# Four cross-attention layers on one core: own orders for the last pairs, low parts on VectorE, an earlier wait for the transposes

## What is computed

```
q = hidden_states @ Wq            # 128 x 1024
k, v = enc @ Wk, enc @ Wv         # 77 x 1024 each
probs = softmax(q k^T / 8 + col_bias)     # per head, 128 x 77
out = (probs @ v) @ Wo + bo + hidden_states
```

## Time and profile before

| | us |
|---|---|
| median of 3 runs | 1819.43 |
| lowest, highest | 1819.06, 1823.53 |
| profiled execution, its own time | 1819.92 |
| its span, first to last instruction | 1817.5 |

### The profile page before, as it was taken

How to read it: one execution, slowest core, us unless ns; L and a number is a source line. 1 busy time by engine, 2 the same in 40 slices (tenths; PEclk the granted TensorE clock), 3 DMA queues, 4 the chain that set the end, 5 groups by cost and what they waited for, 6 DMA issues and landing times.

```text
span 1817.5 us, 72896 instructions
## 1 busy us (share of the span) xinstructions
PE 1760.4 (97%) x28400; PEld 1510.9 (83%) x28400; DVE 1578.3 (87%) x3010; ACT 1471.7 (81%) x2987; POOL 1599.4 (88%) x2136
## 2 busy tenths in 40 slices
PE   6599999999999999999999999999999999999996
PEld 6478888888888888888888888888888888888885
DVE  6689988899889998899888998899888898889983
ACT  4388888888888888888888888888888888888873
POOL 3389999999999999999999998999999999999973
PEclk7599999999999999999999999999999999999998
DMA  5269999999999999999999999998999999999996
GB/s 173 43 134 191 174 181 191 186 185 170 192 185 184 183 171 186 193 179 185 176 187 189 177 187 180 187 188 171 189 183 186 183 174 183 178 170 188 174 186 130
DMA packets 1168210, 320.35 MB, mean 176 GB/s; under 512 B 1140246, under 2 KB 1164124, under 8 KB 1167868
## 3 DMA queue, kind: packets, MB, share of 16 engines
q1 hardware_dynamic: 1167868, 315.69, 94.0%
HBM read 15.93 MB, written 4.19 MB: 11 GB/s over the span
## 4 chain that ended last, share of the span: by engine, by line
PE 90%; issue 1%; DMA 1%; SPq 1%; ACT 0%; DVE 0%; ACTq 0%; DVEq 0%
PE ring L1226 50%; PE sc L1368 12%; PE o_ps L1226 9%; PE o_ps L1386 5%; PE ring L1440 5%; PE sc L1347 4%; PE ring L1297 2%; PE sc L1366 1%; PE ring L1421 1%; PE ring L1437 1%; DMA arena<-p_sm 1%; PE ring L1274 0%; PE o_ps L1382 0%; PE ring L1277 0%; SPq L485 0%
## 5 line engine op out<-in xcount | busy, mean ns | idle before, releaser
L1226 PE MATMUL ring<-ctx_four,m_w 128*128 128x154 f16 x6144 | 461.4, 230 | 1.5 <-ACT o_tf L710 0.9
L1226 PEld LDWEIGHTS ring<-ctx_four,m_w 128*128 128x128 f16 x6144 | 428.8, 96 | 2.5 <-ACT o_tf L710 1.3
L1107 DVE TENSOR_TENSOR arena<-sc,row_max 128x616 f32<-128x616 f32 (+1 forms) x384 | 387.0, 1008 | 7.0
L644 POOL TENSOR_TENSOR p_sm<-arena,p_sm 128x616 f16<-128x616 f32 x256 | 334.6, 1318 | 39.5 <-ACT p_sm L710 38.0
L639 POOL TENSOR_TENSOR p_sg<-arena,p_sg 128x512 f16<-128x512 f32 (+1 forms) x256 | 341.9, 1357 | 2.3 <-ACT p_sg L710 2.3
L710 ACT ACTIVATE arena<-ring 128x462 f16<-128x462 f32 (+1 forms) x384 | 198.9, 518 | 153.9 <-PE ring L1226 153.5
L1086 DVE TENSOR_TENSOR arena<-ring,arena 128x462 f16<-128x462 f32 (+1 forms) x384 | 224.6, 586 | 73.2 <-ACT arena L710 64.2
L1226 PE MATMUL ring<-wv_m,ctx_four 128*103 128x512 f16 (+1 forms) x1152 | 281.1, 380 | 0.9 <-ACT v_all L710 0.9
L671 POOL TENSOR_TENSOR arena<-arena 128x1024 f16<-128x1024 f32 x128 | 272.8, 2131 | 9.3 <-ACT arena L710 9.3
L1368 PE MATMUL sc<-arena,x_s 128*128 128x512 f16 (+1 forms) x1152 | 263.6, 338 | 0.0
L1104 DVE TENSOR_REDUCE row_max<-sc 128x6 f32<-128x462 f32 (+2 forms) x384 | 210.9, 576 | 12.1 <-PE sc L1368 11.5
(11 more groups left out here) (172 smaller groups left out, 3682.0 us busy)
## 6 DMA issues: line engine op xcount, KB each, us to landing
v_fourth<-v_tile SPq DMA_DIRECT2D x64, 105.6 KB
ctx_nat<-in_ctx_dram SPq DMA_DIRECT2D x64, 77.0 KB
x_nat<-in_x_dram SPq DMA_DIRECT2D x64, 64.0 KB, 2.4
arena<-p_sg SPq DMA_TRANSPOSE x256, 3.5
arena<-p_sm SPq DMA_TRANSPOSE x256, 4.4
out_dram<-y_out SPq DMA_DIRECT2D x64, 64.0 KB, 2.2
v_fourth<-v_tile SPq DMA_DIRECT2D x32, 101.6 KB
arena<-in_L_xattn_Wk_dram SPq DMA_DIRECT2D x2, 1024.0 KB, 6.0
```

Of the source, the lines that this page charges most:

```text
L644: pool.tensor_tensor(p_sm[:, k, LO, :, 0:S], probs_m[:, hs, :], p_sm[:, k, HI, :, 0:S], ALU.subtract).then_inc(sems["pm_lo"], 1)
L1107: dve.tensor_tensor(out, s_view[:, hs, :], row_max[:, hs].unsqueeze(2).to_broadcast([P, hs.stop - hs.start, S]), ALU.subtract).then_inc(do ...
L1226: ins = pe.matmul(out, a, b, start=(n == 0), stop=(n == len(passes) - 1))
```

## The change

1. `turn_m(m, first half)` waits for om_raw of item m - 2 with count 1 (14 heads done) and not 2 (all 16). This holds in all rounds. The second half still waits for count 2.
2. `output_m` of layer 3 waits for turned_o after the two residual matmuls, not ahead of them. This too holds in all rounds.
3. `pair(NIT, 0)` stays. `pair(NIT, 1)` to `pair(NIT, 5)` are replaced on SP, ACT, DVE and PE by `last_pair`, with other orders. On POOL `pair` stays.
4. The low parts of items 3 and 5 (`low_part`, two halves each, and `low_out`) go from POOL to DVE (`on_vector`).

SP, and its `last_pair`:

```diff
-                    sp.wait_ge(sems["om_raw"], at("om_raw", it, m - 2, 2))
+                    sp.wait_ge(sems["om_raw"], at("om_raw", it, m - 2, half + 1))
...
+            def last_pair(it, n):
+                m = 2 * n + 1
+                if exists(it, m - 2):
+                    turn_m(it, m - 2, 1)
+                if exists(it, m):
+                    turn_m(it, m, 0)
+                if exists(it, m - 4):
+                    turn_out(it, m - 4)
+                if exists(it, m) and part(m) != 3:
+                    move_values(it, m)
+                if layer(m - 6) == LAYERS - 1 and exists(it, m - 6):
+                    store(it, m - 6)
```

POOL (the same condition stands ahead of the two `low_part`), and then a piece of ACT's `last_pair`:

```diff
-                if exists(it, m - 4):
+                if exists(it, m - 4) and not on_vector(it, m - 4):
                     low_out(it, m - 4)
...
+                if exists(it, m):
+                    exponential_m(it, m, 0)
+                    if n == 1:
+                        high_m(it, m, 0)
+                    exponential_m(it, m, 1)
+                if n > 1 and exists(it, m - 4):
+                    normalise_rest(it, n, m - 4)
+                if n > 1 and exists(it, m):
+                    high_m(it, m, 0)
+                if n > 1 and exists(it, m - 4):
+                    high_out(it, m - 4)
+                if exists(it, m):
+                    high_m(it, m, 1)
+                if n > 1:
+                    last_layer(it, n, m - 6)
```

DVE, and PE's `output_m`:

```diff
+            def low_part(it, m, k):
+
+                hs = slice(k * HALF, (k + 1) * HALF)
+                dve.wait_ge(sems["pm_hi"], at("pm_hi", it, m, k + 1))
+                dve.tensor_tensor(p_sm[:, k, LO, :, 0:S], probs_m[:, hs, :], p_sm[:, k, HI, :, 0:S],
+                                  ALU.subtract).then_inc(sems["pm_lo"], 1)
...
-                pe.wait_ge(sems["turned_o"], at("turned_o", it, m, 16))
...
                 pe.wait_ge(sems["xb"], at("xb", it, m, 1))
                 pe.matmul(ring[:, b, 0:D], x_b[st][:, :], ident_y[:, :], start=True, stop=False)
+                pe.wait_ge(sems["turned_o"], at("turned_o", it, m, 16))
```

99 lines of the change are left out of this document (90 added, 9 removed).

## The result

The changed kernel takes 1823.07 us (median, 1821.76 to 1825.70) beside 1819.91 us for the kernel before on the same chip: ratio 1.0017, 95% interval [1.0011, 1.0024], so about 3.2 us more. The forecast was 1821.0 us, the range 1818.2 to 1823.8 us.

A forecast was written before the change was run, and what follows sets the result against it. TensorE's own pace bounds the rounds; in the last 45 us SyncE's single queue of transposes does. turn_out(5) 1.25 us late, less 0.77 us, is +0.5; one slow transpose at +1.1 makes +1.6: 1821.0 us, range 1818.2 to 1823.8.

The forecast's parts named there:

- The rounds, and the relaxed wait: Before the tail: no effect and no new TensorE wait; in the tail the relaxed wait saves turn_m(5, first) 0.2 to 0.3 us.
- The queue: SyncE's queue in the tail: turn_m(3, second) issued 0.5 us late, turn_out(1) 5.2 us late, turn_out(5) 1.25 us late.
- slow transpose: Tail's chain of seven transposes: one counted as slow, at +1.1 us (bounds: none, 0; two, 2.2).
- The start of the chain: SyncE's queue: item 3's low parts done at 1785.1, turn_m(3, first) at 1784.4, 1.9 us gained; each transpose holds it 1.6 us.
- The landing of turn_m(3, second): Tail: it lands 3.9 us after its issue at 1789.7, at 1793.6, and the 18 matmuls end at 1794.3.
- output_m(1): TensorE's tail: 1.9 us after turn_out(1) lands at 1800.1, part of it at the lower clock; values_m(5) starts after it.
- The last round trip: End of tail: ym_raw at 1809.0 and low_out(5) at 1808.9 release turn_out(5) at 1809.15; early residual matmuls gain 0.77 us.
- Rival A: TensorE's tail: the clock falls earlier, in the new gaps; +2.6 us in all, +2.2 if only at the second gap; 33%.
- B: TensorE's tail: the clock doesn't fall before the last product, so faster than before, -0.8 us, 1818.6 us; 10%.
- C: Tail's chain: two or more slow transposes, or a DVE low part waiting for POOL's low_out(1); +3 to +4 us; 9%.
- Low parts on VectorE: Items 3 and 5 in the tail: 0.80 us per low part, 1.22 us per output low part; POOL's 1.32 and 2.13.

The follow-up runs named there:

- x1_waits: The kernel before with only the relaxed wait for 14 heads and the residual matmuls ahead of the wait, all orders old: ratio 0.9992 to the kernel before.
- x2_out_first: The changed kernel with turn_out of an item issued ahead of turn_m(., first) of the next on SyncE's queue: ratio 1.0001 to the kernel before.
- x9_filled_less: The changed kernel with unused matmuls (14, 24, 4 and 12) ahead of the waits for turn_out of items -1, 1, 3, 5: ratio 1.0013 to the kernel before.
- x5_act_early: The changed kernel with ScalarE doing the older item first and VectorE its last two heads' reciprocal ahead of its maxima: ratio 1.0014 to the kernel before.
- x6_best: The changed kernel with ScalarE's and VectorE's older work first, turn_out ahead of the next turn_m(., first), move_values and stores moved: ratio 0.9982 to the kernel before.
- x3_low_on_pool: The changed kernel with low parts and output low parts of items 3 and 5 back on GpSimd: ratio 1.0022 to the kernel before.
- x12_rest_first: x6_best with item 1's last two heads multiplied ahead of scores_m(5) and their reciprocal earlier on VectorE: ratio 0.9977 to the kernel before.
- x10_best_shifted: x6_best with 92 empty TensorE instructions at the start, dropped in building, so a repetition of x6_best: ratio 0.9987 to the kernel before.
- x13_rest_shifted: x12_rest_first with 28 one-row, one-column matmuls (56 instructions) at the start of TensorE's program: ratio 0.9981 to the kernel before.

## Why the prediction was right in sign and range, and where its steps were off

**The rounds, and the relaxed wait.** Right: no new wait of TensorE, and x1_waits shows that the two edits cost nothing. In the tail turn_m(5, first) waits at the relaxed line for the 18 matmuls, as predicted.

**The queue.** Right in mechanism, and confirmed by x2_out_first: turn_out(-1) behind turn_m(3, first), turn_m(3, second) late though its data is ready, turn_out(1) behind turn_m(5, first). In the prediction's axis (0.69 us added to the times of the changed kernel) turn_m(3, first) went at 1785.05 (1784.4 predicted), turn_out(-1) at 1786.8 (1786.2), turn_m(3, second) at 1790.6 (1789.7), turn_out(1) at 1798.96 (1796.2), turn_out(3) at 1805.7 (1802.5) and turn_out(5) at 1812.5 (1809.15).

**Where 2.3 us were missed.** The tail grew by 3.9 us, the forecast said 1.6. turn_out(5) went 3.35 us behind its place in the forecast's timeline; 1.1 us of that the forecast had apart, as its slow transpose, which leaves 2.25 us. Four terms were mis-sized, all to the same side. (a) The start of the chain, 0.9 us by turn_m(3, second): VectorE had done both low parts of item 3 at 1785.6, not 1785.1, turn_m(3, first) went 0.65 us later, and turn_out(-1) held the queue for 2.12 us instead of 1.6. The durations of the low parts were right (VectorE's rows of the changed kernel, two low parts and one output low part):

```profile
1783.39 1.54 DVE L1267 TENSOR_TENSOR p_sm<-arena,p_sm 128x616 f16<-128x616 f32 x2
...
1803.29 1.22 DVE L1273 TENSOR_TENSOR arena<-arena 128x1024 f16<-128x1024 f32 x1 [6.21 <-ACT arena L728]
```

(b) The landing of turn_m(3, second): 4.2 us, not 3.9. It was so in all seven kernels where move_values and a store are issued right ahead of it (4.18 to 4.29 us). (c) The slow transpose: I added it as one lump of 1.1 us at the end. turn_m(5, first) took 5.24 us to land, 1.4 us over the usual, and held the queue for 3.07 us instead of 1.6, so that turn_out(1), and not only what waits for the landing, came 1.5 us late: 0.4 us over the lump. (d) output_m(1): the forecast put 1.9 us between the landing of turn_out(1) and its end, and it took 2.8 us, since all of it ran at the lower clock; the values of item 5 stand behind it, and the chain that ended last leads through both. That is 0.9 us; 0.3 us of it came back on the way to turn_out(5), where the forecast had allowed more for semaphores and for the second condition. With 0.9, 0.3, 0.4 and 0.6 us that is 2.2 of the 2.25 us.

The last round trip was seen wrongly in one more point. The forecast let both conditions of turn_out(5) meet, the output product of item 3 at 1809.0 and the low part at 1808.9. output_m(3) ran at full clock in 1.51 us and was done at 1810.2 us in the changed kernel's own time, the low part at 1811.6: the second alone released it.

Term (c) is no property of the change. In its repetition no transpose of the tail was slow, and turn_out(5) still went 3.6 us later than before. There the 18 matmuls ahead of turn_m(5, first) ran at the lower clock, 1.17 us instead of 0.73. And the kernel before had slow transposes on its own chain (turn_m(5, first) took 5.0 and turn_m(5, second) 4.7 us; x1_waits without them is 0.7 us earlier at turn_out(5)), which the forecast did not set against its own 1.1 us. That the time still fell into the range is owed to its width.

**Rival A.** Its mechanism came true: the clock fell at the end of the gap from 1786.7 to 1790.0 us, as the Trainium skill says in "TensorE: Matmul & The Clock Gate" (HAM oscillation) of gaps between bursts that wait for a DMA; this trace agrees. Its price was about right: of the two terms that I put for it, the 18 matmuls (0.5 us) are there in the repetition (0.44 us) and not in the change's trace, and output_m(1) (0.7 us) is there in both (0.9 us). The estimate from x9_filled_less is 1.1 us in sum. The forecast, which had the clock at full until 1800, I gave 45%, and A 33%; by the profile A was what happened, and its +2.6 us lie nearer to the measured 3.2 us than the forecast's +1.6 us.

**Rivals B and C.** The last product took 2.74 us, so B is out. The time, 3.2 us over before, lies in the band of C (+3 to +4), but neither of C's mechanisms is in the profile: one transpose of the chain was slow, none in the repetition, and VectorE's low parts did not wait for GpSimd's low_out(1), which started at 1792.15, between them.

**What I did not see.** ScalarE's order. I took high_out(1) to be done in time because turn_out(1) was queued late anyway; that was true for this kernel, and the reason why x5_act_early gained so little, but it is half of what the change gives away against x6_best.

**Low parts on VectorE.** Their durations were right to 0.02 us, and the gain of 1.9 us at turn_m(3, first) was counted against the kernel before, where move_values stood in front of it. x3_low_on_pool, where turn_m(3, first) goes at the same point with GpSimd's low parts, shows that the engine had no part in it.

## What to carry to other kernels

In a queue that issues in order, put an issue whose data is ready early ahead of one that waits for newer work, and look at each engine's own order for the second such inversion: it shows only when the first is mended. A faster engine for a step pays only where that engine doesn't have to wait for the step's input. The edits here are worth at most 7 us in 1820, and a single profile of the same program moves a named instruction by 1 us, by where an instruction packet falls beside a transpose and in which stretch the clock is low. So judge such an edit by both, the place of a named instruction and the median of many runs, and repeat the kernel that the conclusion rests on.

## What the runs showed of the hardware

**A transpose with an instruction packet in its flight takes longer.** q8 has 228 packets of 16 KB (227 in two of the traces), TensorE 58,309 instructions: one packet for each 256. In the tails of the fourteen traces (from 1770 us on) I could pair 142 transposes of 512 KB with issue and landing. The 103 with no packet from 0.5 us ahead of their issue to their landing took 3.63 to 4.29 us; the 16 with a packet 0.9 to 2.8 us after their issue all took 4.87 to 5.72 us. Of the other 23, which had a packet at another time, 17 took 4.2 us or less. The slower six: two with a packet 0.5 and 0.7 us after their issue (4.5 us), three right behind a long one with the packet at their issue (4.7 to 5.1 us), and turn_out(1) of x12_rest_first (packet 3.4 us after the issue, 5.65 us). So the expectation of x10_best_shifted, that all transposes of over 4.9 us had their packet 0.9 to 2.7 us after the issue, was too simple. With ten of the sixteen, that issue or the next held the queue for 2.6 to 3.6 us instead of 1.6.

The rounds agree. From 110 to 1765 us of the fourteen traces, turn_m (arena<-p_sm) had a median of 4.03 us without a packet (1,509 of them) and 5.30 us with one 0.9 to 2.8 us after the issue (534); turn_out (arena<-arena) 3.79 us (492) and 5.38 us (404). Two comparisons go beyond such a count: x13_rest_shifted moved the packets by about 53 instructions and turn_out(1) became 1.5 us shorter, and in the two executions of the changed program the same transpose took 5.2 us with the packet 1.2 us behind its issue and 3.8 us with it ahead.

**The clock.** The 24 matmuls of an output product took 1.51 us at 2.4 GHz and 2.74 us at 1.2 GHz, the 18 matmuls of 128x65 0.73 and 1.17 us. In two executions of one program the clock fell at the same gaps but not for the same stretches: 18.7 to 22.1 and 25.5 to 35.7 us in for the change, 17.2 to 24.0 and 27.4 to 34.3 us in for its repetition.

**Padding at the start.** 56 instructions that ran in 0.84 us, in time in which TensorE was idle, went with a start of the tail 2.9 us later in the one profiled execution; about 1.3 us of that lie outside the scatter of the other kernels, and the cause isn't shown.
